# The fourteen norms of a twelve-layer model: variance to reciprocal root on GpSimd in place of ScalarE and VectorE

## The reference

```
x = x + L0_xattn(layernorm(x), ctx)     x = x + L0_attn(layernorm(x))    x = x + L0_ffn(layernorm(x))
x = x + L1_xattn(layernorm(x), ctx)     x = x + L1_attn(layernorm(x))    x = x + L1_ffn(layernorm(x))
x = x + L2_xattn(layernorm(x), ctx)     x = x + L2_attn(layernorm(x))    x = x + L2_ffn(layernorm(x))
x = x + L3_xattn(layernorm(x), ctx)     x = x + L3_attn(layernorm(x))    x = x + L3_ffn(layernorm(x))

def layernorm(x, eps=1e-05):
    m, v = mean(x, -1), var(x, -1)
    return (x - m) / sqrt(v + eps)
```

## Time and profile before

| | us |
|---|---|
| median of 3 runs | 2767.6 |
| lowest and highest of the 3 | 2760.06, 2772.73 |
| the profiled execution's own time | 2774.48 |
| its span | 2772.7 |
| mean granted TensorE clock | 0.977 of full speed |

### The profile page before, as it was taken

The page is one execution under the profiler, slowest core; times in us unless marked ns, Lnnn a source line. Parts: engine busy times, 40 slices in busy tenths (PEclk is TensorE's granted clock), DMA queues, the critical chain, the costliest instruction groups (busy, mean ns, idle before and its releaser), DMA issues. The chain is left out here.

```text
span 2772.7 us, 47692 instructions
## 1 busy us (share of the span) xinstructions
PE 2593.5 (94%) x18722; PEld 1955.1 (71%) x18722; DVE 1466.6 (53%) x2389; ACT 994.4 (36%) x2147; POOL 631.7 (23%) x657
## 2 busy tenths in 40 slices
PE   8889997999999898979999998979999999998999
PEld 4566994666666657948888877967888884576645
DVE  3474224777777732035555556235555553599851
ACT  2252224666666322322222221213222222577430
POOL 2002002000101001013333322023333330078541
PEclk9999998999999998999999998999999999999999
DMA  9443873111110105932211203733211111022200
GB/s 289 126 136 111 302 263 92 47 32 42 37 32 17 50 1 174 326 112 65 67 60 58 69 18 126 265 121 96 69 60 63 62 35 40 24 85 84 80 0 16
DMA packets 97806, 260.08 MB, mean 94 GB/s; under 512 B 19028, under 2 KB 45369, under 8 KB 90185
## 3 DMA queue, kind: packets, MB, share of 16 engines
q1 hardware_dynamic: 86520, 240.17, 26.2%
q0 software_dynamic: 3840, 10.49, 1.2%
q10 hardware_dynamic: 7248, 6.65, 0.7%
HBM read 236.13 MB, written 21.14 MB: 93 GB/s over the span
## 5 line engine op out<-in xcount | busy, mean ns | idle before, releaser
L2184 POOL TENSOR_TENSOR buf<-buf 128x512 f32<-128x512 f32 x128 | 159.9, 1271 | 504.8 <-ACT buf L2318 504.8
L2343 DVE TENSOR_REDUCE buf<-acc 128x256 f32<-128x1024 f32 x128 | 150.8, 1220 | 219.0 <-PE acc L2211 219.0
L2244 PE MATMUL acc<-buf 128*128 128x256 f32 x1024 | 257.2, 384 | 3.6 <-ACT buf L2327 3.6
L2205 PE MATMUL acc<-buf 128*128 128x256 f32 x1024 | 236.6, 384 | 3.5 <-PEq L89 2.6
L2205 PEld LDWEIGHTS acc<-buf 128*128 128x128 f32 x1024 | 189.4, 190 | 36.9 <-issue 12.1
L2312 ACT COPY buf<-acc 128x256 f32<-128x256 f32 x64 | 23.8, 372 | 533.5 <-PE acc L2226 533.5
L2244 PEld LDWEIGHTS acc<-buf 128*128 128x128 f32 x1024 | 180.8, 190 | 37.5 <-issue 15.9
L2712 ACT ACTIVATE buf<-acc,buf 128x512 f32<-128x512 f32 x256 | 172.4, 685 | 75.3 <-DVE buf L2746 75.3
L2746 DVE TENSOR_REDUCE buf<-acc 128x1 f32<-128x512 f32 x256 | 159.0, 683 | 65.1 <-PE acc L2624 65.1
L2356 DVE TENSOR_TENSOR buf<-acc,buf 128x1024 f32<-128x1024 f32 x128 | 150.8, 1220 | 67.8 <-ACT buf L2312 67.8
L2636 PEld LDWEIGHTS acc<-identity,buf 128*128 128x128 f32 x1024 | 115.0, 141 | 84.0 <-issue 78.2
(11 more groups left out here) (420 smaller groups left out, 4851.4 us busy)
## 6 DMA issues: line engine op xcount, KB each, us to landing
buf<-in_L_ffn_W SPq DMA_DIRECT2D x52, 1024.0 KB, 6.6
buf<-in_ctx SPq DMA_DIRECT2D x48, 768.0 KB, 4.3
buf<-in_ctxT SPq DMA_DIRECT2D x64, 512.0 KB, 3.9
buf<-in_L_ffn_w SPq DMA_DIRECT2D x36, 704.0 KB, 5.6
buf<-state_rows SPq DMA_DIRECT2D x32, 512.0 KB, 3.5
buf<-in_ctxT SPq DMA_DIRECT2D x96, 128.0 KB, 4.0
buf<-in_L_ffn_w SPq DMA_DIRECT2D x18, 640.0 KB, 6.4
buf<-in_ctxT SPq DMA_DIRECT2D x32, 256.0 KB, 5.2
```

Of the source, the lines that this page charges most:

```text
L2184: pool.tensor_tensor(quarters[:, 2 * n:2 * n + 2, :], t[:, 4 * n:4 * n + 2, :], t[:, 4 * n + 2:4 * n + 4, :], ALU.add).then_inc(adding, 1)
L2205: pe.matmul(acc_s[:, n, :], ct0[x][:, tile(key_tile(n))], q0[:, b, 4 * y:4 * y + 4, :], start=(n % 2 == 0), stop=False)
L2244: pe.matmul(acc_m[:, 0:ROWS], ctx[x][:, key_tile(n), 0:P], probsT[y][:, n, :], start=(n == 0), stop=(n == KT - 1))
L2343: dve.tensor_reduce(most_of[n][:, :], acc_s[:, 4 * n:4 * n + 4, :].rearrange("p k r -> p r k"), AX.X, ALU.max).then_inc(part_most, 1)
```

## The change

`Statistics.root` goes from ScalarE's list to GpSimd's. There it takes two instructions of 128 by 8: an addition of eps, then a `tensor_tensor` with the operation pow, whose second operand is a tile filled with -0.5. Its result is already the reciprocal root, so VectorE's reciprocal is dropped. The memory for eps becomes that for the exponents. All stages that hold a norm get a GpSimd list for it, or have it at the end of the one they had. ScalarE's `root` calls go.

```diff
     def close(self, dve):
         n, c = self.n, Chain(dve, self.measured, 2 * NT)
-        dve.wait_ge(self.rooted, 1)
-        c.link(dve.reciprocal(n.rstd[:, :], n.std[:, :]))
+        dve.wait_ge(self.rooted, 2)
         if self.twice:
 ...
-            dve.wait_ge(self.rooted, 2)
-            c.link(dve.reciprocal(n.rstd2[:, :], n.std[:, :]))
+            dve.wait_ge(self.rooted, 4)
 ...
-    def root(self, act):
+    def root(self, pool):
         n = self.n
-        act.wait_ge(self.measured, 2 * NT)
-        act.activation(n.std[:, :], n.mv[:, :, 1], ACT.Sqrt, bias=n.eps[:, 0:1]).then_inc(self.rooted, 1)
+        pool.wait_ge(self.measured, 2 * NT)
+        pool.tensor_scalar(n.spread[:, :], n.mv[:, :, 1], EPS, None, ALU.add).then_inc(self.rooted, 1)
+        pool.wait_ge(self.rooted, 1)
+        pool.tensor_tensor(n.rstd[:, :], n.spread[:, :], n.minus_half[:, :], ALU.pow).then_inc(self.rooted, 1)
         if self.twice:
-            act.wait_ge(self.measured, 2 * NT + 3)
-            act.activation(n.std[:, :], n.var[:, :], ACT.Sqrt, bias=n.eps[:, 0:1]).then_inc(self.rooted, 1)
+            pool.wait_ge(self.measured, 2 * NT + 2)
+            pool.tensor_scalar(n.spread[:, :], n.var[:, :], EPS, None, ALU.add).then_inc(self.rooted, 1)
+            pool.wait_ge(self.rooted, 3)
+            pool.tensor_tensor(n.rstd2[:, :], n.spread[:, :], n.minus_half[:, :], ALU.pow).then_inc(self.rooted, 1)
 ...
-            dve.memset(chip.norm.eps[:, :], 1e-5).then_inc(eps_set, 1)
+            dve.memset(chip.norm.minus_half[:, :], -0.5).then_inc(half_set, 1)
```

More of the change, by code:

```diff
@@ L21 @@
 HALF = 512
+EPS = 1e-5
 LANDINGS = ((0, 1), (2, 3), (4, 5), (6,), (7,))
@@ L158, in close @@
                                             op0=ALU.mult, op1=ALU.mult))
-    def root(self, act):
+    def root(self, pool):
         n = self.n
-        act.wait_ge(self.measured, 2 * NT)
-        act.activation(n.std[:, :], n.mv[:, :, 1], ACT.Sqrt, bias=n.eps[:, 0:1]).then_inc(self.rooted, 1)
+        pool.wait_ge(self.measured, 2 * NT)
+        pool.tensor_scalar(n.spread[:, :], n.mv[:, :, 1], EPS, None, ALU.add).then_inc(self.rooted, 1)
+        pool.wait_ge(self.rooted, 1)
+        pool.tensor_tensor(n.rstd[:, :], n.spread[:, :], n.minus_half[:, :], ALU.pow).then_inc(self.rooted, 1)
         if self.twice:
-            act.wait_ge(self.measured, 2 * NT + 3)
-            act.activation(n.std[:, :], n.var[:, :], ACT.Sqrt, bias=n.eps[:, 0:1]).then_inc(self.rooted, 1)
+            pool.wait_ge(self.measured, 2 * NT + 2)
+            pool.tensor_scalar(n.spread[:, :], n.var[:, :], EPS, None, ALU.add).then_inc(self.rooted, 1)
+            pool.wait_ge(self.rooted, 3)
+            pool.tensor_tensor(n.rstd2[:, :], n.spread[:, :], n.minus_half[:, :], ALU.pow).then_inc(self.rooted, 1)
 class Norm:
     def __init__(self, sb):
-        self.mv, self.eps = sb(P, NT, 2), sb(P, 1)
-        self.var, self.std, self.rstd, self.shift, self.rstd2, self.shift2 = (sb(P, NT) for _ in range(6))
+        self.mv = sb(P, NT, 2)
+        self.spread, self.minus_half, self.var, self.rstd, self.shift, self.rstd2, self.shift2 = (sb(P, NT) for _ in range(7))
 def idle_products(chip, pe, acc, n):
@@ L282, in _ @@
                 then["act"](act, done)
-            if statistics:
-                statistics.root(act)
         @block.tensor
@@ L318, in _ @@
                 idle_products(chip, pe, turned[0][0], 4)
-        if "pool" in work:
+        if "pool" in work or statistics:
             @block.gpsimd
             def _(pool):
-                work["pool"](pool)
+                if "pool" in work:
+                    work["pool"](pool)
+                if statistics:
+                    statistics.root(pool)
 def matmul_jobs(chip, jobs, loads, setup=None, nbanks=6, then=None, stats=None, twice=False, ahead=(), also=None, first=None):
@@ L406, in _ @@
                 statistics.close(dve)
-        if "pool" in then:
+        if "pool" in then or statistics:
             @block.gpsimd
             def _(pool):
-                then["pool"](pool, done)
+                if "pool" in then:
+                    then["pool"](pool, done)
+                if statistics:
+                    statistics.root(pool)
 def rows(r):
@@ L2077, in load_tokens @@
     with Stage(chip) as st:
-        zeroed, eps_set, ident_in = st.sems(3)
+        zeroed, half_set, ident_in = st.sems(3)
         x_in = st.sems(4)
@@ L2092, in _ @@
             statistics.close(dve)
[L2094 to L2097, removed]
+        @block.gpsimd
+        def _(pool):
+            pool.wait_ge(half_set, 1)
+            statistics.root(pool)
         @block.tensor
```

## The result

| | before | after |
|---|---|---|
| median of 4 runs, us | 2770.16 | 2799.73 |
| lowest and highest | 2760.06, 2774.41 | 2796.66, 2802.64 |
| the profiled execution's own time | 2774.48 | 2802.64 |
| its span | 2772.7 | 2800.8 |
| time at TensorE's lower clock (1.2 GHz) in it, summed from the trace, us | 130 | 161 |

The ratio is 1.0117, with a 95% interval from 1.0094 to 1.0140: slower by 30 us by the medians, and by 26 to 39 us by the interval. The forecast was 2787 us, 19 more than the median then known (2767.6, of three runs; a fourth has come since), in a range from 2768 to 2812.

A forecast was written before the change was run, and what follows sets the result against it. TensorE is busy 94% of the span, but norms stand on the path: 14.4 + 0.5 + 0.9 + 1.3 = 17.1 us, plus 2 for the clock, on 2767.6 gives 2787 us. Range 2768 to 2812, the forecast's own 2780 to 2798.

The forecast's parts named there:

- The bound: At the norms, root and reciprocal lie on every engine's path, 0.61 us from last aggregation to shift; two norms partly covered.
- X: At each norm, the duration of GpSimd's power instruction of 128 by 8: 1.4 us, between 1.1 and 2.0.
- 70 steps: Inside the power instruction, chosen from 40 to 100 counted steps at 17 ns each, over a fixed 0.18 us.
- The rest of the chain: At each norm, GpSimd's wake-up, the addition of eps and two handovers around the power: 0.41 us together.
- The two norms with cover: At 433 and 1206 us TensorE's idle products outlast the norm by 0.72 and 1.65 us, so they add 0.5 and 0.
- The first norm and L0_attn: A table load comes onto the path before ScalarE's first normalisation, 1.0 us, and before L0_attn's own root, 1.3 us.
- The twelve loads that go: ScalarE's table loads of 1.283 us lie in its idle time, so removing them gains nothing; rival on the path, chance 0.03.
- The clock: Behind norms, TensorE's longer stops add one to two falls to 1.2 GHz, up to 1.7 us each: 2 us.
- my sign of one or two more: In the changed kernel's profile, half-clock periods should be one or two more; five or more would make a separate cause.
- The rival in which it falls at every norm: Behind all norms the clock falls, fourteen times 1.7 us, 24 in place of 2, giving 2809 us; chance 0.05.
- 14 X - 2.5: Whole kernel, the added time in us around the chosen power duration, without the clock's share.
- the row's 1.4: The power's duration in us, from a GpSimd product's 2.1 ns a column, 17 ns a step on 8 columns.

The follow-up runs named there:

- the second profile of the changed kernel: The changed kernel unchanged, run again in five rounds on one slower chip beside the kernel before: 2813.47 us, ratio 1.0116.

## Why the prediction came out as it did

- **The bound.** Right: the exchange lies on the path at every norm, in part at the two with cover. VectorE's wait was forecast at 1.8 us a norm and is 2.12.
- **X.** Forecast 1.4 from 70 steps, measured 1.67: right in kind, and small by 0.27 us, 3.8 us in the sum. The step count was a guess from no row, and that it came near is luck: the slope of 0.159 us a column is 75 times the 2.1 ns that a further column costs a product, but no run shows that the power works in such steps. The fixed part was what I had too small, 0.18 against 0.40.
- **The rest of the chain.** Forecast 0.41 us, measured 0.45: the wake-up was right at 0.08, the addition takes 0.24 to 0.25 instead of 0.21. That is 0.6 us in all.
- **The two norms with cover.** Forecast 0.5 us and 0 more. From aggregation to the next block it went from 2.11 to 2.91 and from 3.04 to 3.19, +0.8 and +0.15, with X larger by 0.27: right. The cover differs between executions: in the second profile of the changed kernel the same two take 3.20 and 2.89.
- **The first norm and L0_attn.** Forecast 1.0 and 1.3 us for the loads, measured 1.01 and 1.28, and both went when the loads were brought forward.
- **The twelve loads that go.** Counted at nothing, and shown to be that. The 32 us that the Trainium skill's price for a switch ("ScalarE: Activation LUTs", "What ACT_TABLE_LOAD costs") would give for all of them, taken as on the path, did not come. The load itself is 1283 ns, as the page says; in L0_attn, where a load stood on the path, the wait grew by these 1.28 us alone, with no drain of 1.38 beside it.
- **The clock.** This is the term that was mis-sized. I had 2 us, one or two falls. The profile has the lower level right behind 8 of the 14 norms, 31 us more of it in all, and 6 us of time for it. The separate periods are 22 now and were 20, which my sign of one or two more would have let pass; they are longer, and their number was the wrong thing to count. The edit that shortens the stop, and nothing else, gave 7.5 us on one chip and 15 on another. I had argued from one stretch with TensorE busy for 1.37 of 3.40 us and the clock kept. That was one case; with stops of 2.2 to 2.3 us some norms keep the clock (those at 223, 958 and 1671 us of the changed kernel's profile) and others lose it (116 and 2324, and with 3.30 and 2.62 us of stop 995 and 2662). The rival in which it falls at every norm, 24 us, was too dear in its turn.
- **The sum.** 14 X - 2.5 with X = 1.67 is 20.9; 0.6 for the chain makes 21.5, against 19.7 + 2.3 = 22.0 in the ledger. 7.5 for the clock, by the first pair of chips, makes 29.0; with the ledger's own 6.1 it is the 28.1 of the profiled pair. Measured 29.6 by medians. Forecast 17.1 + 2. All three misses, X, the chain and the clock, have the same sign, so the time lies 2 us above the range that I gave the forecast itself (2780 to 2798), though X lies inside its own (1.1 to 2.0) and the time inside the outer range.

The Trainium skill's rule for dependent operations ("GPSIMD Engine Reference", "Performance pitfalls for Q7 kernels") had given X = 2.05 by my 70 steps. The measured 1.67 lies between it and the row's 1.4, and since the number of steps is my own, no run decides on the rule.

## What to carry to other kernels

A short operation on a path that every engine waits at must be priced with its wake-up and its fixed part, not by its place on an idle engine: here 12 fewer table loads on ScalarE's idle time bought nothing, and 1.5 us at each of 14 barriers cost 30 in all, clock and two moved loads included. Where TensorE waits behind that path, a delay costs more than its length, because the clock may fall for the work that follows. If such a delay can't be avoided, fill the stop with products that end with it, and count their passes first.

## What the runs showed that I had not expected

- GpSimd's power on 128 partitions takes 0.56, 0.715, 1.354 and 1.667 us for 1, 2, 6 and 8 columns.
- Removing a function can bring a table load onto another one's path: the norm's root had left its table for L0_attn's.
- 24 us of added waiting cost 30 to 36 us, and between 7 and 15 us of the change's loss came back by products of zeros alone.
- TensorE had the lower clock for 2.3 us in the first 6 us behind the 14 norms with stops near 0.8 us, for 28.6 with stops near 2.3, and for 52.9 with stops near 4.0.
